# Spreading a tile's normalised rows, slot numbers and probabilities over the column groups: transfers inside SBUF in place of selector products

## What is computed

```python
xn = _layernorm(x)
x = x + gnn(xn) + mix(xn)
x = x + memory(_layernorm(x))

def memory(x, Wq, bq, keys, w_down, w_up):          # 8 heads, 256 keys per half, top 8
    q = (x @ Wq + bq).reshape(-1, 8, 128)
    q1, q2 = q[..., :64], q[..., 64:]
    s1 = einsum('bhc,hnc->bhn', q1, keys[:, 0]);  s2 = einsum('bhc,hnc->bhn', q2, keys[:, 1])
    s1t, i1 = top_k(s1, 8);  s2t, i2 = top_k(s2, 8)
    scores, best = top_k(s1t[..., :, None] + s2t[..., None, :], 8)     # of 64 pairs
    indices = take_along_axis(i1[..., :, None] * 256 + i2[..., None, :], best)
    inner = einsum('bd,bhkd->bhk', x, w_down[indices])                 # 64 rows per token
    vals = relu(inner) * softmax(scores)
    return einsum('bhk,bhkd->bd', vals, w_up[indices])
```

## Time and profile before

| | us |
|---|---|
| three runs | 2688.16, 2706.21, 2712.06 (median 2706.21) |
| profiled execution, its own time | 2709.85 |
| its span, first to last instruction | 2708.0 |
| PE busy | 2263.9 (84%) |
| DVE busy | 1451.2 (54%) |
| POOL busy | 1037.5 (38%) |
| ACT busy | 739.0 (27%) |

### The profile page before, as it was taken

One profiled execution on the slowest core, in us unless ns is written; L12 is line 12 of the kernel. 1 busy time (PEld: TensorE's weight loads), 2 busy tenths in 40 slices (PEclk: granted clock), 3 DMA queues, 4 the chain that ended last, 5 costly groups with the idle time before them and its releaser, 6 DMA issues.

```text
span 2708.0 us, 29597 instructions
## 1 busy us (share of the span) xinstructions
PE 2263.9 (84%) x10300; PEld 1284.7 (47%) x10300; DVE 1451.2 (54%) x3903; ACT 739.0 (27%) x1837; POOL 1037.5 (38%) x886
## 2 busy tenths in 40 slices
PE   3999989997799999999999877787887778877543
PEld 2656656664344444444765644444444434444200
DVE  3765674455466500001334158666776777767674
ACT  1345231210110001000446223333334333343222
POOL 0046877771111100000000026555655555555665
PEclk9999999998899999999999888887988889887755
DMA  9934144449566530432023238888988888888998
GB/s 300 286 90 129 2 121 114 94 104 220 195 186 182 152 75 0 116 104 75 1 31 125 62 129 308 296 300 288 318 303 292 319 297 316 299 300 305 341 362 317
DMA packets 242915, 531.73 MB, mean 196 GB/s; under 512 B 103774, under 2 KB 105173, under 8 KB 238611
## 3 DMA queue, kind: packets, MB, share of 16 engines
q0 software_dynamic: 170032, 379.99, 43.2%
q1 hardware_dynamic: 64413, 144.24, 17.5%
q10 hardware_dynamic: 8330, 5.71, 0.7%
HBM read 493.10 MB, written 48.92 MB: 200 GB/s over the span
## 4 chain that ended last, share of the span: by engine, by line
PE 66%; DVE 16%; issue 7%; DMA 5%; another core or an unknown queue 3%; ACT 2%; POOL 1%; SPq 0%; DVEq 0%; ACTq 0%
PE bank L1147 13%; PE bank L1124 5%; PE bank L1461 4%; PE bank L980 4%; PE bank L991 4%; PE bank L1478 4%; PE bank L1469 4%; PE bank L1353 3%; PE bank L748 3%; PE bank L650 3%; PE bank L671 3%; PE bank L1134 2%; PE bank L658 2%; DMA stage<-xn_d 2%
## 5 line engine op out<-in xcount | busy, mean ns | idle before, releaser
L1322 POOL DMA_INDIRECT qv<-in_L_ffn_rows,qv x162 | 162.6, 1003 | 809.0 <-DVE qv L1733 672.4
L1616 ACT ACTIVATE stage<-stage,qv 128x32 f32<-128x32 f32 x640 | 203.0, 320 | 495.1 <-issue 191.4
L310 POOL DMA_INDIRECT adj<-e_cnt,e_idx x80 | 172.0, 2150 | 214.9 <-issue 183.7
L1461 PEld LDWEIGHTS bank<-stage,big 128*128 128x128 f32 x1280 | 184.2, 214 | 107.7 <-issue 79.3
L1461 PE MATMUL bank<-stage,big 128*128 128x125 f32 x1280 | 196.9, 303 | 28.6 <-ACT stage L1583 24.4
L1322 POOL DMA_INDIRECT big<-in_L_ffn_rows,qv x160 | 163.7, 1023 | 139.2 <-PE bank L1478 96.1
L1322 POOL DMA_INDIRECT ring_more<-in_L_ffn_rows,qv x159 | 162.0, 1019 | 126.7 <-PE bank L1478 80.8
L310 POOL DMA_INDIRECT adj_b<-e_cnt,e_idx x80 | 163.7, 2046 | 46.9 <-issue 26.0
L1322 POOL DMA_INDIRECT h<-in_L_ffn_rows,qv x159 | 158.2, 995 | 50.2 <-issue 44.8
L1478 PE MATMUL bank<-big,stage 128*32 128x512 f32 x320 | 144.7, 761 | 38.3 <-issue 27.6
L1478 PE MATMUL bank<-ring_more,stage 128*32 128x512 f32 x318 | 140.5, 749 | 39.2 <-ACT stage L1616 20.3
(11 more groups left out here) (259 smaller groups left out, 4109.1 us busy)
## 6 DMA issues: line engine op xcount, KB each, us to landing
wreg<-in_L_gnn_basis SPq DMA_DIRECT2D x30, 1024.0 KB
stage<-in_L_gnn_basis POOLq DMA_DIRECT2D x45, 512.0 KB, 4.4
big<-in_L_mix_W SPq DMA_DIRECT2D x4, 4096.0 KB
adj<-adj_b POOLq DMA_DIRECT2D x9, 1328.1 KB, 25.5
adj<-wreg SPq DMA_DIRECT2D x5, 2187.5 KB
adj_b<-wreg SPq DMA_DIRECT2D x5, 2187.5 KB
wreg<-adj SPq DMA_DIRECT2D x10, 1093.8 KB
qv<-adj SPq DMA_DIRECT2D x10, 1093.8 KB
```

Of the source, the lines that this page charges most:

```text
L310: nc.gpsimd.indirect_dma_start(out=(adj, adj_b)[g % 2], out_offset=bass.IndirectOffsetOnAxis(ap=e_idx[:, g:g + 1], axis=0), in_=e_cnt[:, g ...
L1322: nc.gpsimd.indirect_dma_start(out=ring[place(t, s)], out_offset=None, in_=a["L0_ffn_rows"], in_offset=bass.IndirectOffsetOnAxis(ap=slots_ ...
L1461: mm = nc.tensor.matmul(psum[F_BANKS[n % 2]][:, 0:P], w1_sb[:, k, 128 * n:128 * n + 128], y1_t[:, k, :], start=(k == 0), stop=(k == KC - 1))
L1616: nc.scalar.activation(wsel[:, s % DRING, :], mask, ACT.Relu, scale=inner[:, s:s + 1]).then_inc(p_diag, 1)
```

## The change

PE's spreads, their selectors, ACT's copies of `xrep` and DVE's copies out of PSUM are removed. In their place SP issues 48 transfers from SBUF to SBUF per tile: 16 for the slots (four blocks e for each of four groups g), 16 for the probabilities, 16 for the rows. A slot or probability transfer has 32 rows of 16 values (29 rows for the last group, since the tile has 125), a row transfer 32 rows of 512 values. DVE writes slot numbers and probabilities in an order by e first, the numbers cast to integers, so that a transfer's 16 values lie side by side; `column(s)` gives the column of a step in the spread lists. `xl` has two buffers, filled up to 128 partitions with zeros. SP waits for the slots (`p_found`), then for the probabilities, then for the dot that last reads a group of `xrep`; this stands at the end of a tile's round in SP's list, ahead of the next round's loads. POOL waits for all 16 slot transfers, dot 0 for all slot and probability transfers, dots 0 to 3 for the four transfers of their group. PE's scores of head 0 wait for the search of the tile before.

```diff
@@ (views)
-        xl = view(qv, 0, [DIM], P)
+        xl_of = [view(qv, 0, [DIM], P), view(qv, 9600, [DIM], P)]
+        xl_rows = [view(qv, 0, [DIM]), view(qv, 9600, [DIM])]
...
+        slot_i = qv[0:P, 3712:3712 + SLOTS].bitcast(I32)
+        prob_e = view(qv, 3776, [SLOTS], P)
...
+        SPREAD = 16 * 16
-        SPREAD_AT = [TAIL_AT + 10, TAIL_AT + 11, TAIL_AT + 14, TAIL_AT + 15]
+        def column(s):
+            return SLOTS // 4 * (s % 4) + s // 4
...
@@ def mem_sp(sp):
+            def x_spread(t):
+                sp.wait_ge(p_x, t + 1)
+                for g in range(4):
+                    if t:
+                        sp.wait_ge(p_dot, t * SLOTS - 3 + g)
+                    else:
+                        sp.wait_ge(p_keysT, 1)
+                    for e in range(4):
+                        sp.dma_start(xrep[WIDE * e:WIDE * e + WIDE, g, :], xl_rows[t % 2][WIDE * g:WIDE * g + WIDE, :]).then_inc(s_xrep[g], 16)
+
+            def spread(to, what, done):
+                for g in range(4):
+                    count = min(WIDE, P - WIDE * g)
+                    for e in range(4):
+                        sp.dma_start(to[WIDE * e:WIDE * e + count, 16 * g:16 * g + 16],
+                                     what[WIDE * g:WIDE * g + count, 16 * e:16 * e + 16]).then_inc(done, 16)
+
+            def slots_spread(t):
+                sp.wait_ge(p_found, 2 * t + 1)
+                if t:
+                    sp.wait_ge(p_slots, SPREAD * t)
+                spread(slots_of[t % 2], slot_i, p_slots)
+                sp.wait_ge(p_found, 2 * t + 2)
+                if t:
+                    sp.wait_ge(p_probs, SPREAD * t)
+                spread(probs_of[t % 2], prob_e, p_probs)
...
             sp.wait_ge(s_h, 16)
+            x_spread(0)
+            slots_spread(0)
             for t in range(TILES):
...
+                if t + 1 < TILES:
+                    slots_spread(t + 1)
+                    x_spread(t + 1)
@@ def mem_pool(pool):
-                pool.wait_ge(p_slots, 2 * t + 1)
+                pool.wait_ge(p_slots, SPREAD * (t + 1))
...
-                        in_offset=bass.IndirectOffsetOnAxis(ap=slots_of[t % 2][:, s:s + 1], axis=0)).then_inc(s_row[place(t, s)], 16)
+                        in_offset=bass.IndirectOffsetOnAxis(ap=slots_of[t % 2][:, column(s):column(s) + 1], axis=0)).then_inc(s_row[place(t, s)], 16)
@@ def mem_pe(pe):
                     elif t:
-                        pe.wait_ge(p_xr, 4 * t)
+                        pe.wait_ge(p_top, (t - 1) * TOPN + 4 * PKH)
...
-            def spread_x(t, g):
-                if g >= 2:
-                    pe.wait_ge(p_xr, 4 * t + g - 1)
-                nc.tensor.matmul(psum[3 + g % 2][:, :], selx[:, g, :], xl, start=True, stop=True).then_inc(p_xr_pe, 1)
-
-            def spread_slots(bank, what):
...
-            def behind(t):
...
@@ def mem_act(act):
-            def spread_x(t, g):
-                act.wait_ge(p_xr_pe, 4 * t + g + 1)
-                if t:
-                    act.wait_ge(p_dot, t * SLOTS - 3 + g)
-                nc.scalar.activation(xrep[:, g, :], psum[3 + g % 2][:, :], ACT.Copy).then_inc(p_xr, 1)
...
@@ def top(dve, t):
-            if t:
-                dve.wait_ge(p_found_pe, 2 * t - 1)
-            nc.vector.scalar_tensor_tensor(slot_f, pick_a, float(NKEYS), pick_b, ALU.mult, ALU.add).then_inc(p_found, 1)
+            nc.vector.scalar_tensor_tensor(slot_f, pick_a, float(NKEYS), pick_b, ALU.mult, ALU.add).then_inc(p_top, 1)
+            n += 1
+            dve.wait_ge(p_top, n)
+            nc.vector.tensor_copy(slot_i.rearrange("p (e s) -> p s e", e=4), slot_f.rearrange("p (s e) -> p s e", e=4)).then_inc(p_found, 1)
...
-            for _ in range(5):
-                yield
-            dve.wait_ge(p_found_pe, 2 * t + 1)
-            nc.vector.tensor_copy(slots_of[t % 2].rearrange("p (s g) -> p s g", g=4), psum[3][:, 0:SLOTS].rearrange("p (g s) -> p s g", g=4)).then_inc(p_slots, 1)
-            yield
-            dve.wait_ge(p_found_pe, 2 * t + 2)
-            nc.vector.tensor_copy(probs_of[t % 2].rearrange("p (s g) -> p s g", g=4), psum[4][:, 0:SLOTS].rearrange("p (g s) -> p s g", g=4)).then_inc(p_slots, 1)
...
@@ def norm3(t), dot(t, s):
-                if t:
-                    dve.wait_ge(p_xr_pe, 4 * t)
-                nc.vector.tensor_scalar(xl, h_of(t), mv[:, t, 0:1], rs[:, 0, t:t + 1], ALU.subtract, ALU.mult).then_inc(p_x, 1)
+                nc.vector.tensor_scalar(xl_of[t % 2], h_of(t), mv[:, t, 0:1], rs[:, 0, t:t + 1], ALU.subtract, ALU.mult).then_inc(p_x, 1)
...
                 if s == 0:
-                    dve.wait_ge(p_slots, 2 * t + 2)
+                    dve.wait_ge(p_slots, SPREAD * (t + 1))
+                    dve.wait_ge(p_probs, SPREAD * (t + 1))
                 if s < 4:
-                    dve.wait_ge(p_xr, 4 * t + s + 1)
+                    dve.wait_ge(s_xrep[s], XREP_FROM[s] + 64 * (t + 1))
```

More of the change, by code:

```diff
@@ L1029, in build @@
         g_sem = [{n: sem(f"gcn{gl}_{n}") for n in g_names[0:13 if gl else 11]} for gl in range(2)]
-        s_gx = [sem(f"gcn0_x_{j}") for j in range(2)]
+        s_gx = [sem(f"x_rows_{j}") for j in range(2)]
         s_slab = [[sem(f"gcn{gl}_slab_{j}") for j in range(2)] for gl in range(2)]
@@ L1240, in build @@
         LAG = 1
+        SELS = 7
+        SPREAD = 16 * 16
         X_AT = 1
@@ L1529, in mem_pe @@
                 pass
-            pe.wait_ge(p_sel, 2)
-            for _ in behind(0):
-                pass
             for t in range(TILES):
                 ahead = front(t + 1) if t + 1 < TILES else iter(())
-                found = behind(t + 1) if t + 1 < TILES else iter(())
                 later = itertools.chain(attend(t + PRE), mlp(t + PRE)) if t + PRE < TILES else iter(())
                 for s in range(SLOTS):
-                    if s == 0:
-                        spread_x(t, 2)
-                        spread_x(t, 3)
-                    for _ in range(SPREAD_AT.count(s)):
-                        next(found, None)
                     for _ in range((s == TURN_AT) + QUERY_AT.count(s) + SCORE_AT.count(s)):
@@ L1839, in mem_dve @@
                 nc.vector.memset(iota8[:, n:n + 1], float(n)).then_inc(m["ln2"], 1)
-            nc.vector.tensor_copy(selx.rearrange("p g (e m) -> p g e m", e=4),
-                                  ident[0:P, :].rearrange("p (g m) -> p g m", g=4).unsqueeze(2).to_broadcast([P, 4, 4, WIDE])).then_inc(p_sel, 1)
+            for rows in xl_rows:
+                nc.vector.memset(rows[96:128, :], 0.0).then_inc(p_sel, 1)
+            for n in range(2):
+                nc.vector.memset(slots_of[n], 0).then_inc(p_sel, 1)
+                nc.vector.memset(probs_of[n], 0.0).then_inc(p_sel, 1)
             nc.vector.tensor_reduce(mask, ident[:, :].rearrange("p (g m) -> p m g", g=4), AX, ALU.add).then_inc(p_sel, 1)
```

42 lines of the change are left out of this document (11 added, 31 removed).

## The result

The changed kernel takes 2836.29 us (median of 2822.50, 2836.29 and 2837.28) against 2706.21: ratio 1.048, 95% interval 1.041 to 1.055. It is slower, as forecast, but by 130 us and not by 44, and it lies above the range that was to hold it.

A forecast was written before the change was run, and what follows sets the result against it. Eight tiles of some 114 us follow TensorE with DMA close behind, the last two DMA. 12 + 8 x 3 + 8 = 44 us on the profiled 2709.85 gives 2754, less 3.6 for the median: 2750; range 2668 to 2805.

The forecast's parts named there:

- what the change frees: Per handover, PE's removed spreads and DVE's two waits (2.76 and 4.46 us) bring dot 1 3.2 to 5.5 us earlier.
- SP's back-to-back issues are 0.32 us apart: SP's queue: each of the 48 transfers per tile takes 0.32 us to issue, 5.1 us for each sixteen.
- rival "SP becomes the bound": At 0.95 us per issue, rows leave SP 46 us after F (start of L1719), dot 1 near F+42: 2870; chance 0.06.
- signs that were to show the forecast right: Probability transfers end about 17 us or more after L1719; dot 1 after F+25; first gather waits for slots; DVE's waits change.
- the one engine: Group 3's 29-row transfers run on one DMA engine, 140 pieces per sixteen, each 0.19 us beside gathers.
- first tile: No older tile's gathers give cover: slots land at F+9.6, dot 0 up to F+25; 12 us lost, bounds 7 and 17.
- steady handovers: From one tile to the next, dot 1 at F+27 to F+32 against F+24.7: 3 us later each, bounds 0 and 7.
- last handover: In the DMA-bound stretch: first gather 3.4 us later, row packets 2.7, ring full some 2: 8 us.
- dot 1 as the mark: At each handover, a delay of dot 1 shifts the whole next tile, through norm3 and PE's transposes and query matmuls.
- Probabilities F+22.8 to F+31: Probability pieces queue behind slots and go one by one with the new gathers, ending at F+22.8 to F+31.
- 3 us to the first packet: From a transfer's issue on SP to its first packet: 3 us, read from a load (2.4 at least).
- rival "faster": Probabilities land before F+19, dot 1 comes 4 us earlier eight times: -26 us, 2680; chance 0.22.

The follow-up runs named there:

- e7: Changed kernel with slot block e of token m on partition 4m + e, one transfer per column group, 12 issues per tile; ratio to the kernel before 0.994.
- e9: Slots and probabilities as in e7, rows by PE and ACT as in the kernel before, 8 issues per tile; ratio to the kernel before 0.993.
- trains: Changed kernel with 8 or 12 transfers of one form issued together behind its last store, queues idle; 0.60 to 0.64 us per small SBUF-to-SBUF issue; total time not compared.
- e1: Changed kernel with 32 rows in place of 29 in group 3's transfers, still 48 issues per tile; ratio to the kernel before 1.040.
- e4: Changed kernel with rows spread by PE and ACT again, slots and probabilities still by transfers, 32 issues per tile; ratio to the kernel before 1.023.
- e8: As e4, but with 32 rows in group 3's transfers; ratio to the kernel before 1.010.
- e2: Changed kernel with slots and probabilities of a block sent in one transfer, 32 issues per tile, 29 rows kept; ratio to the kernel before 1.011.
- e5: Kernel before with only the rows spread by transfers, 16 per tile; slots and probabilities still by selector products; ratio to the kernel before 1.012.

## Why the prediction was right and wrong

**Right: what the change frees.** The MLP's last product comes 4.1 us earlier (L1786 at F+13.6, median, against F+17.7), and DVE's two waits are gone; 3.2 to 5.5 were given and 4 taken. In e7 and e9 that gain reaches dot 1.

**The step that failed: "SP's back-to-back issues are 0.32 us apart (out, then h) ... I take 0.32".** It is 0.63 (trains), and 0.66 to 0.71 in the handover shown. The two rows it was read from the earlier trace rows have 125 rows and an end in DRAM; a transfer with both ends in SBUF is another form, and the key loads' 0.95, set aside as an upper bound, was the sign that the price is not one figure (it is a mean itself: nine of the sixteen last 0.47 us, seven 1.04 to 1.93). The forecast reasoned by size ("These have 32, so I take 0.32"); from one element to 32 rows of 2 KB inside SBUF the price does not depend on it. With 0.63 the prediction's own working has slots leave by F+10.6, probabilities by F+20.7, rows by F+31; in the nine handovers of the trace the probabilities have left SP by F+20.6 to F+22.5, the rows by F+31.6 to F+33.5. The rival "SP becomes the bound", given 0.06, was the mechanism; the measured point lies between it and the forecast, dot 1 at F+34 and not at F+42.

The signs that were to show the forecast right all came: 17 us or more to the end of the probability transfers, DVE idle before dot 0, dot 1 after F+25, the first gather waiting for slots, the two waits gone. They would have come under the SP rival as well, so they do not tell the two apart; when SP's issues end does. And the direction was right for another reason than the one given: without the one engine (e1) 4.0 of the 4.8% stay.

**The sum, term by term**, in the profiled executions (2820.6 - 2708.0 = 112.6 us):

| term | predicted | measured | how |
|---|---|---|---|
| first tile | 12 (7 to 17) | 22.7 | dot 0 of tile 0 at 1623.17 against 1600.45 |
| steady handovers | 8 x 3 (0 to 7 each) | 66.4 | eight periods between dots 0, mean 122.8 against 114.5 |
| last handover | 8 | 23.4 | last period 122.4 against 93.3, less 5.7 won back until the end |

The first row takes in that F came 1.9 us earlier in this execution: from F the first tile loses 24.6. All three are out mainly for the one reason: each hangs on when SP's sixteenth, thirty-second and forty-eighth issue leaves. At both ends the one engine adds to it: with 32 rows (e1) dot 0 comes 6.2 us earlier in the first tile and 10.0 in the last.

**Right, but small: the one engine.** One completion for 29 rows, as foretold. It is worth some 0.9% in the changed kernel (e1) and 1.3% where rows do not hide it (e4 to e8); the forecast built most of its delay on it. Its price of a piece beside gathers, 0.19 us, is what e4 shows. The counts it was read from, 518 and 519, could not show it: two queues that take turns of any equal length leave equal counts. That all the 29-row transfers of a sixteen stand on the same engine, which the 140 pieces take, no run shows outright; in e4's handover at F = 2183.24 the last 56 pieces, nearly two such transfers, leave one at a time over 10 us, as they would on one engine. The pieces beside gathers cost most where the issues were late: in e7, with all engines, the probabilities leave SP before the new gathers do, and dot 0 does not wait for them.

**Half right: dot 1 as the mark.** The forecast followed dot 1 and stopped. Dots 2 and 3 each wait for their own group; in the changed kernel dot 3 is 12.0 us late where dot 1 is 9.1. In all twelve kernels of the table the change of the period lies between the shift of dot 1 and that of dot 3, or within 0.5 us of one of them: + 9.7 us with + 9.1 and + 12.0 (changed), + 1.1 with - 0.9 and + 2.8 (e2), + 2.4 with + 2.5 and + 5.4 (e5), - 2.0 with - 4.2 and - 1.9 (e7). Which of the two sets it in a given kernel, no run here separates.

**Luck: "Probabilities F+22.8 to F+31".** The last 64-byte piece of a tile goes out at F+23.7 to F+31.7 in the eight handovers up to tile 8, F+25.3 in the one shown. The range fits, but it was worked out from pieces that queue on one engine from F+13 on, and SP had not issued the last of them before F+20.6: with 32 rows (e1) the last still goes out at F+24.7 to F+26.5. Dot 0, at F+31.2 in the handover shown, had to wait longer, for the first row group.

**Right in the handovers: 3 us to the first packet.** Beside the old tile's gathers the first 64-byte piece leaves 2.0 to 3.8 us after the start of the first issue. In the first tile, where no gathers run, it is 1.2 us, as in the idle trains (inside SBUF; from DRAM 0.9, to DRAM 0.8), so there the 3 was too long by nearly 2.

**The rival "faster"** needed probabilities before F+19. With 48 issues they cannot leave by then; with 12 they do, and e7 shows its gain, though 17 us (0.6%) and not 26.

## What to carry to other kernels

Count the transfers before the bytes: each one costs its queue a price that goes by the form of the transfer (here some 0.63 us inside SBUF, from one element to 64 KB, and 0.45 for 32 rows with an end in DRAM), and a burst of them is late by its number times that. Whether a second engine's queue could take a part of the burst was not tried. Choose the layout so that one transfer writes all 128 partitions, and count the completions of a transfer in the trace before relying on all engines (here 16 for 32 and 128 rows, 5 for 125, one for 29, and 4 for a source of [4, 32, 512] into 128 partitions). Take the price of an instruction only from a row of the same form, and where the trace has none, let the upper bound decide the range.
